# Two attention items in flight, projections one unit ahead, row normalisation moved to ScalarE

## The reference

```python
x = L0_attn_hidden_states
xn = _layernorm(x, axis=-1)
s = _L0_attn_ref(xn, L0_attn_wq, L0_attn_wk, L0_attn_wv, L0_attn_wo)
g = _silu(_L0_ffn_ref(xn, L0_ffn_router_w, L0_ffn_A, L0_ffn_B))
x = x + s * g
...
q = q * cos + _rotate_half(q) * sin
k = k * cos + _rotate_half(k) * sin
...
scores = scores * scale
scores = scores + causal.astype(dt)
probs = jax.nn.softmax(scores.astype(jnp.float32), axis=-1).astype(dt)
attn = jnp.einsum('bhqk,bhkd->bhqd', probs, v)
```

## Time and profile before

| | |
|---|---|
| time, median of 3 runs | 1474.9 us (1472.89 to 1476.49) |
| span of the profiled execution | 1473.0 us |
| PE matmul busy | 1372.8 us (93%) |
| DVE busy | 1196.0 us (81%) |
| ACT busy | 809.3 us (55%) |
| POOL busy | 423.0 us (29%) |

### The profile page before, as it was taken

The page is one execution under the profiler, slowest core; times in us unless marked ns, Lnnn a source line. Parts: engine busy times, 40 slices in busy tenths (PEclk is TensorE's granted clock), DMA queues, the critical chain, the costliest instruction groups (busy, mean ns, idle before and its releaser), DMA issues.

```text
span 1473.0 us, 23326 instructions
## 1 busy us (share of the span) xinstructions
PE 1372.8 (93%) x6982; PEld 1130.1 (77%) x6982; DVE 1196.0 (81%) x3022; ACT 809.3 (55%) x2064; POOL 423.0 (29%) x340
## 2 busy tenths in 40 slices
PE   6699999999998999989999999999999999999997
PEld 5577667788777887778777887778877787877785
DVE  6976768878889887888888788887787888888887
ACT  4445555555555665556555555556555565555563
POOL 4311123221434123241342213331233312423231
PEclk9799999999999999999999999999999999999999
DMA  5000021000001000000000000000000000001223
GB/s 196 22 12 1 22 72 65 22 7 0 21 21 28 0 7 21 14 28 0 14 28 21 7 0 21 21 28 0 2 26 14 28 0 14 22 13 64 79 71 136
DMA packets 23291, 43.33 MB, mean 29 GB/s; under 512 B 2464, under 2 KB 2592, under 8 KB 23264
## 3 DMA queue, kind: packets, MB, share of 16 engines
q1 hardware_dynamic: 20736, 37.90, 8.0%
q10 hardware_dynamic: 2528, 5.11, 0.9%
HBM read 34.61 MB, written 8.39 MB: 29 GB/s over the span
## 4 chain that ended last, share of the span: by engine, by line
PE 49%; issue 21%; DVE 18%; POOL 8%; ACT 3%; DMA 0%; POOLq 0%; DVEq 0%; ACTq 0%
PE o_ps L542 13%; PE bank_b L450 12%; PE bank_a L450 7%; PE s_ps L517 5%; PE pv_ps L532 4%; POOL rot L366 3%; DVE probs L1126 3%; PE t_ps L625 3%; POOL w_lo L359 3%; DVE probs L1079 2%; POOL w_hi L356 2%; PE s_ps L512 2%; DVE cosx L999 2%; DVE cosx L989 2%; DVE q_lo L1005 2%
## 5 line engine op out<-in xcount | busy, mean ns | idle before, releaser
L366 POOL TENSOR_TENSOR rot<-rot,tab 128x512 f32<-128x512 f32 x160 | 209.6, 1310 | 921.3 <-ACT rot L730 921.3
L800 ACT ACTIVATE probs<-probs,row_min 128x128 f32<-128x128 f32 (+1 forms) x512 | 227.1, 445 | 122.1 <-DVE row_min L1079 120.9
L1126 DVE TENSOR_SCALAR probs<-probs,row_inv 128x128 f32<-128x128 f32 (+1 forms) x512 | 208.5, 470 | 4.5
L450 PE MATMUL bank_b<-xT_hi,w_hi 128*128 (+1 forms) x508 | 205.3, 404 | 0.5 <-POOL w_lo L373 0.5
L542 PE MATMUL o_ps<-w_hi,attn_hi 128*128 128x512 f32 x500 | 198.9, 398 | 7.2 <-POOL w_lo L359 4.0
L450 PE MATMUL bank_b<-xT_hi,w_lo 128*128 (+1 forms) x508 | 199.8, 393 | 0.0
L450 PE MATMUL bank_b<-xT_lo,w_hi 128*128 (+1 forms) x508 | 199.2, 392 | 0.0
L542 PE MATMUL o_ps<-w_lo,attn_hi 128*128 128x512 f32 x500 | 197.3, 395 | 0.0
L542 PE MATMUL o_ps<-w_hi,attn_lo 128*128 128x512 f32 x500 | 196.8, 394 | 0.0
L761 ACT ACTIVATE attn_hi<-pv_ps 128x512 fp32r<-128x512 f32 x128 | 76.4, 597 | 172.1 <-PE pv_ps L532 171.3
L625 PE MATMUL t_ps<-tab,probs 128*128 128x128 f32 x768 | 110.9, 282 | 49.1 <-DVE probs L1126 49.0
(11 more groups left out here) (151 smaller groups left out, 3094.8 us busy)
## 6 DMA issues: line engine op xcount, KB each, us to landing
raw<-w_seq SPq DMA_DIRECT2D x78, 256.0 KB, 2.6
gate_scratch<-silu ACTq DMA_DIRECT2D x16, 256.0 KB, 2.1
out<-y_sum SPq DMA_DIRECT2D x16, 256.0 KB, 2.0
raw<-x SPq DMA_DIRECT2D x13, 256.0 KB, 2.7
raw<-gate_scratch SPq DMA_DIRECT2D x13, 256.0 KB, 2.9
x_sb<-x SPq DMA_DIRECT2D x3, 1024.0 KB, 10.6
x_sb<-x SPq DMA_DIRECT2D x4, 256.0 KB, 5.7
tab<-tables ACTq DMA_DIRECT2D x1, 768.0 KB, 5.3
```

Of the source, the lines that this page charges most:

```text
L366: nc.gpsimd.tensor_tensor(v, v, tab[:, s:s + SEQ].unsqueeze(1).to_broadcast([P, 2, SEQ]), ALU.mult).then_inc(sin_done[kind], 1)
L450: mm = nc.tensor.matmul(dst, w(a, c), x[:, c, bass.ds(x0, BLOCK)], start=(c == 0 and n == 0), stop=(c == DC - 1 and n == 2))
L800: a = nc.scalar.activation(s, s, ACT.Exp, bias=row_min[:, i:i + 1], scale=-1.0, accum_out=row_sum[:, i:i + 1])
L1126: ins = nc.vector.tensor_scalar(s, s, row_inv[:, i:i + 1], None, ALU.mult)
```

## The change

The bank pairs `s_ps` and `t_ps` become `pair[0]` and `pair[1]`: the scores of item j and its turned rows share `pair[j % 2]`, and `probs` and `row_min` are doubled. So scores are made two items ahead. All six projections of a unit are made in the unit before. The output tile follows two items behind, not three. The four row normalisations per item move from DVE (`tensor_scalar`) to ACT (`normalise_rows`, an activation with the row's inverse as its scale). K's high part and V's parts are made in one instruction each, not two. The gate steps stand only at places 0 and 3 of an item (after the turning, and at the item's end), over units 0 to 5, and seven units are written out.

```diff
+WRITTEN = 7
...
-        places = [(0, 1, 3)] + [(0, j, p) for j in (2, 3) for p in (0, 1, 3)]
...
+        later = [(u, j, p) for u in range(2, WRITTEN) for j in range(4) for p in (0, 3)]
...
-        s_ps = pb("s_ps", [P, 2, 512])
-        t_ps = pb("t_ps", [P, 2, 512])
+        pair = [pb("pair0", [P, 2, 512]), pb("pair1", [P, 2, 512])]
```

POOL's `group`:

```diff
-                        if i == 0 and j == 2:
-                            pool.wait_ge(proj_done[VT1], own)
-                            split(g, WO)
-                            split(g, WO + 1)
-                        if j > 0 and not last:
-                            sin_product((K, H0)[j - 1] if j < 3 else H1, ahead)
...
+                        if j == 1:
+                            if i == 0 and not first:
+
+                                pool.wait_ge(o_done, value(pool, 4 * u0))
+                                split(g, WO)
+                            if not last:
+                                sin_product(H0, ahead)
+                            if i == 0 and not first:
+                                split(g, WO + 1)
+                            if not last:
+                                sin_product(H1, ahead)
...
+                        if (i, j) == (2, 1):
                             pool.wait_ge(proj_done[K], used)
                             split(g_next, WK)
...
+                            pool.wait_ge(proj_done[H0], used)
+                            split(g_next, WQ)
+                        elif (i, j) == (2, 2):
...
+                            split(g_next, WQ + 1)
+                        elif (i, j) == (2, 3):
...
+                            split(g_next, WQ + 2)
                             pool.wait_ge(proj_done[H3], used)
                             split(g_next, WQ + 3)
```

TensorE's item j of a unit:

```diff
+                pe.wait_ge(probs_ready, n4[j + 1])
+                turn_probs(j)
                 pe_side(u, j, 0)
...
+                        project(K, bank_a, WK, x_next, w_next)
...
+                        project(H1, bank_a, WQ + 1, x_next, w_next)
...
+                        project(H3, bank_a, WQ + 3, x_next, w_next)
...
+                        project(V, bank_b, WV, x_next, w_next)
+                pe_side(u, j, 1)
+
+                pe.wait_ge(pT_ready, n4[j + 1])
+                if j < 2 or not last:
+                    if j == 2:
                         for kind in (K, H0, H1):
                             pe.wait_ge(q_ready[kind], c2)
...
+                    scores((j + 2) % 4)
...
+                prob_value(j)
...
+                    output_heads(b, t, o_ps, range(GROUP), weights=w_own if j == 2 else None).then_inc(o_done, 1)
...
+                        project(H0, bank_b, WQ, x_next, w_next)
...
+                        project(H2, bank_b, WQ + 2, x_next, w_next)
...
+                pe_side(u, j, 3)
```

ScalarE:

```diff
+        def normalise_rows(j, done):
+            act = nc.scalar
+            act.wait_ge(inv_done, done)
...
+                    a = nc.scalar.activation(s, s, ACT.Copy, scale=row_inv[:, i:i + 1])
+            a.then_inc(probs_ready, 1)
...
+                if j == 1 and not last:
+                    k_high(c2, n4[4])
+                    q_high(H0, c2, n4[3])
...
+                if not end:
+                    normalise_rows((j + 1) % 4, n4[j + 2])
```

VectorE:

```diff
-                        ins = nc.vector.tensor_scalar(s, s, row_inv[:, i:i + 1], None, ALU.mult)
-                ins.then_inc(probs_ready, 1)
...
+                elif j == 1 and not last:
+                    rotate(H0, c2)
+                    cos_product(H1, bank_a, c2)
```

More of the change, by code:

```diff
@@ L61, with loop @@
 KINDS = ["k", "h0", "h1", "h2", "h3"]
-BUF = {K: 0, H0: 1, H1: 0, H2: 1, H3: 1}
-V, VT0, VT1 = 5, 6, 7
+BUF = {K: 0, H0: 1, H1: 0, H2: 1, H3: 0}
+V = 5
+WRITTEN = 7
+FINAL = UNITS - BLOCKS
+LAST = UNITS - 1
+def loop(eng, first, end, body):
+    with eng.Fori(first, end) as i:
+        body(i)
 def build(nc, x, w_seq, a_r, b_t, tables, out):
@@ L154, in build @@
         x0_in = [sem(f"x0_in{t}") for t in range(BLOCK_TILES)]
+        land_in = [sem(f"land_in{c}") for c in range(len(landing))]
         ar_in = sem("ar_in")
@@ L238, in build @@
             through_ps += what in THROUGH
-        assert len(places) >= len(steps)
-        SIDE_X = TILES - X_FIRST
+        assert all(at < (3, 2, 0) for at, (what, _, _) in side_plan.items() if what in ("x", "ar", "mt", "route", "exp"))
         def side_uses(u, j, p):
@@ L279, in value, with slots, units @@
             return v if isinstance(v, int) else eng.snap(v)
+        def slots(eng, u):
+            return {c: value(eng, 4 * u + c) for c in range(-2, 8)}
+        def units(eng, u):
+            return [value(eng, u + c) if c else u for c in range(3)]
         @block.sync
@@ new lines, in group @@
+                        if g_next is None and 4 * i + j > 2:
+                            add_residual(4 * i + j - 3, (4 * i + j - 3) % 2)
+                        if j == 0 and not last:
+                            sin_product(K, ahead)
+                        if j == 0 and i == 0 and first:
+                            inverse_std(2)
+                        if j == 1:
[8 more added lines that the diff above has]
+                                sin_product(H1, ahead)
+                            if i == 0 and first:
+                                inverse_std(3)
+                                split(g, WO)
+                                split(g, WO + 1)
@@ new lines, in act_unit @@
+                if j == 1 and not last:
+                    k_high(c2, n4[4])
+                    q_high(H0, c2, n4[3])
+                elif j == 2 and not last:
+                    q_high(H2, c2, n4[4])
+                if not end:
+                    normalise_rows((j + 1) % 4, n4[j + 2])
+                attn_high(j, n4[j + 1], None if first and j < 3 else n4[(-2, -2, 0, 0)[j]])
+                act_side(u, j, 2)
+                act_side(u, j, 3)
+                if is_unit(u, last_d[0]) and j == last_d[1]:
+                    store_silu(TILES - 1)
@@ L1094, in dve_unit @@
-                dve_side(u, j, 0)
-                if j == 0:
-                    q_low(H2, c1)
-                    if first:
-                        for t in range(BLOCK_TILES, 2 * BLOCK_TILES):
-                            x_low(t, first_banks[t % BLOCK_TILES])
-                elif j == 2 and not last:
-                    k_low(0, c2)
-                elif j == 3 and not last:
-                    q_low(H0, c2)
-                if not (first and j == 0):
-                    turned_low(n)
@@ L1157, in dve_unit @@
-                dve_side(u, j, 2)
+                elif j == 3 and not last:
+                    q_low(H3, c2)
+                if not end:
+                    row_inverse(n4[j + 2])
+                if j == 0 and not last:
+                    cos_product(K, bank_a, c2, H3, c1)
+                elif j == 1 and not last:
+                    rotate(H0, c2)
+                    cos_product(H1, bank_a, c2)
+                elif j == 2 and not last:
+                    rotate(H2, c2)
+                    cos_product(H3, bank_a, c2, H1, c2)
@@ new lines, in dve_unit @@
+                if first and j == 0:
+                    block_statistics(2)
+                elif first and j == 1:
+                    block_normalise(2)
+                    block_statistics(3)
+                elif first and j == 2:
+                    block_normalise(3)
+                if is_unit(u, 1) and j == 2:
+                    split_ar()
+                dve_side(u, j, 1)
+                if j < 2 or not last:
+                    mask_rows((j + 2) % 4, n4[j + 3])
+                if j == 0 and not last:
+                    rotate(K, c2)
+                elif j == 1 and not last:
+                    k_low(c2)
+                    q_low(H0, c2)
+                    rotate(H1, c2)
+                elif j == 2 and not last:
+                    q_low(H2, c2)
+                    rotate(H3, c2)
```

763 lines of the change are left out of this document (345 added, 418 removed).

## The result

The changed kernel takes 1561.8 us (median of 4 runs, 1560.98 to 1563.99) where the kernel before takes 1474.9: 1.0597 times as long, 95% interval 1.0582 to 1.0612. The forecast was 1535, slower, in a range of 1455 to 1575. The direction was right and 27 us were missing. The profiled execution has a span of 1559.2 us, and what follows is reckoned on it.

What follows compares the result with a forecast made beforehand. TensorE was taken as nearly matmul-bound, losing time where weights are split. First turning 43.5, units 0 to 6 378, units 7 to 30 1072 and end 39.5 gave 1533 us span, 1535 median; range 1455 to 1575.

Steps and rivals of the forecast that it cites:

- Clean unit: Unit without weight splits: 39.7 us of matmul stream plus 1.4 waiting for H1's low part, 41.1 (40.6 to 41.5).
- First unit: First unit of a group: POOL's sine behind a split awaiting the output tile costs 11 us over clean (6.5 to 13).
- ScalarE's normalisation: Four row normalisations per item moved from DVE to ScalarE: 1.4 us there, between 1.0 and 2.0.
- Third unit: Third unit of a group, where five chunks are split: 4 us over a clean unit, bounds 1 and 7.
- The rival in which the port costs little: DVE slips between POOL's instructions; first unit costs 6.5, third 1 to 2, gate 66: 1480 to 1495 us; chance 0.20.
- The rival in which the clock falls in each unit: The 1.4 us wait in every unit lowers TensorE's clock, losing 1.7 us each: 1578 us; chance 0.08.
- The gate: Gate steps in units 0 to 6: 56 us before plus 1.1 for each of 19 pairs, 77 (56 to 95).
- The first turning: Stretch from the start to TensorE's first turning: 43.5 us, as before.
- The last unit: Last unit and end, without projections to hide the parts behind: 39.5 us, where 38.1 before.

Runs made afterwards that it cites:

- Experiment 1: Changed kernel, with POOL making H0's and H1's sine products before it waits for the output tile and splits two output chunks in a group's first unit: 1503.5 us.
- experiment 2: Changed kernel with the four row normalisations back on DVE, directly behind the reciprocal: 1591.8 us.
- mended kernel: Kernel 9: (8) with the next group's splits K in third unit, H0 to H3 in fourth's long items, V in its item 2; routing in unit 3: 1467.2 us.
- (11): The mended kernel with the four row normalisations back on DVE: 1494.2 us.
- (3): The kernel before, with only the four row normalisations moved to ScalarE, directly after the exponentials: 1576.8 us.
- (5): Experiment 1 with the last twenty gate steps at places 0 and 1 of an item, not 0 and 3: 1496.9 us.
- (8): Experiment 1 with all gate steps but one at places 0 and 1, x's first transposes one item later, first gate tiles one item after routing: 1479.5 us.
- Kernel 12: The mended kernel with K's split in item 0 of the third unit, H0's behind K's sine product, V's in item 1 of the fourth: 1472.5 us.

## Why the forecast was right in direction and 27 us short

**Clean unit: right.** 41.1 forecast, 41.1 measured. In a clean unit's item 2, DVE's low part of H1 and the scores that wait for it:

```profile
918.38 1.28 POOL L361 TENSOR_TENSOR rot<-rot,tab 128x512 f32<-128x512 f32 x1 [6.71 <-ACT rot L713]
...
919.01 1.19 DVE L1003 TENSOR_TENSOR q_lo<-cosx,q_hi 128x512 fp32r<-128x512 f32 x1
...
920.35 0.36 PE L515 MATMUL pair<-k_parts,q_hi 128*128 128x256 f32 x1 [1.36 <-DVE q_lo L1003]
```

POOL's sine ends at 919.66 and DVE's subtraction 0.54 later, 1.19 us long where 0.7 is the mean in the kernel before. The Trainium skill (SBUF — State Buffer, Who interferes with whom) says that a VectorE instruction with two SBUF inputs contends with a GpSimd instruction that reads SBUF, and the trace agrees again: 4 of the 128 low parts of Q took over 0.9 us in the kernel before and 37 in the changed one, and POOL was at work at the start of every one of them.

**First unit: right, link by link.** ScalarE, DVE and POOL from item 1 of a first unit on:

```profile
860.08 1.04 POOL L346 TENSOR_TENSOR w_hi<-raw,zero 128x512 fp32r<-128x512 f32 x1 [13.67 <-PE o_ps L544]
861.20 1.29 POOL L349 TENSOR_TENSOR w_lo<-raw,w_hi 128x512 fp32r<-128x512 f32 x1
862.45 1.26 POOL L361 TENSOR_TENSOR rot<-rot,tab 128x512 f32<-128x512 f32 x1
```

```profile
865.28 0.63 ACT L720 ACTIVATE q_hi<-cosx 128x512 fp32r<-128x512 f32 x1 [7.00 <-DVE cosx L997]
865.82 1.48 ACT L767 ACTIVATE probs<-probs,row_inv 128x128 f32<-128x128 f32 x4
```

```profile
863.74 1.51 DVE L997 TENSOR_TENSOR cosx<-cosx,rot 128x512 f32<-128x512 f32 x1 [7.39 <-POOL rot L361]
...
870.77 1.80 DVE L1003 TENSOR_TENSOR q_lo<-cosx,q_hi 128x512 fp32r<-128x512 f32 x1
```

TensorE's turning of item 1 is at 851.36. From there: the split begins at 8.7 (forecast 8.7), the rotation ends at 13.9 (14.0), ScalarE's normalisation at 15.9 (16.0), TensorE has stood 4.72 us (4.8). The scores come at 877.42, which is 26.1 (near 26), after 4.84 us (some 6; the projection before them ran partly at the lower clock). The unit costs 11.8 over a clean one (11). Experiment 1 shows that the order makes 8.8 of it.

Of the 11.8 us, 8.2 are longer waits (4.72, and 4.84 where a clean unit has 1.37). The remaining 3.6 go with the lower clock: over this unit the granted clock is 0.90, where it is 1.00 in kernel 1's first unit and in a clean one. So some 3.6 of the 8.8 us that the bad order costs are the clock that falls with the waits, of which the prediction counted 1.6 (an estimate by subtraction).

How much of the second wait is contention and how much is DVE's late start was not measured apart.

**ScalarE's normalisation: right.** 1.4 forecast, 1.48 measured, and the Trainium skill's rule (ScalarE: Activation LUTs, Rules for kernel authors) that multiplications belong on VectorE costs 30 us here when it is followed (experiment 2) and 27 in the mended kernel (11). In the kernel before it is right by 102 us (3). As the traces read, which engine is the better one depended on what stood behind the instruction in the queue, not on its length.

**Third unit: right,** 4.3 of 4. **The rival in which the port costs little** falls: in the first unit the rotation and the low part of H0 met POOL and took 1.51 and 1.80 us, and even without the bad order (experiment 1) such a unit costs 3 us over a clean one. **The rival in which the clock falls in each unit** falls too: the granted clock is 1.00 from 893 to 945, through a whole clean unit with its wait of 1.36. In the loop it falls only in first and third units (0.950 over the whole run, where the kernel before has 0.972).

**The gate: the term that was mis-sized.** At the loop's prices units 0 to 6 come to 7 x 41.15 - 5.6 + 11.8 + 2 x 4.3 = 302.9, so the gate cost 394.7 - 302.9 = 92 us, where the sum had 77 and its upper bound 95. I counted 1.1 us for each pair of steps and nothing for what stands ahead of a step in DVE's queue. The pair itself was sized right: at 225.58 and 228.20 the two steps wait 0.35 and 0.69 us. But setting ten pairs apart (5) brought 4.5 us in units 0 to 6 and not 12, so what remains of the 92 is not all pairs. Three steps waited for DVE's queue (TensorE, wait in brackets):

```profile
75.67 0.69 PE L456 MATMUL o_ps<-tab,x_sb 128*128 128x128 f32 x2 [10.05 <-DVE xT_lo L903]
...
214.10 1.03 PE L491 MATMUL o_ps<-tab,mid 128*64 128x128 f32 x4 [11.44 <-DVE mid L980]
...
319.91 1.22 PE L495 MATMUL o_ps<-bT_full,gmT_full 64*128 64x512 f32 x1 [10.64 <-DVE y_sum L1061]
```

The first stands behind DVE's statistics and norms, the second behind the routing, the third, in the first unit of a group, behind the rotation that waits for POOL: there the wait of the loop's first unit and the gate's pair fall on each other. The three make 32 us; in the kernel before, the longest such waits were 5.1 and 1.9. Moving the steps apart (8) and the routing to a unit without splits, together with the new places of the splits (9), brought units 0 to 6 from 380.8 in kernel 1 to 361.4 and 351.1, the time of the kernel before.

**The small terms.** The first turning came at 45.2, not 43.5: its normalisation now stands behind ScalarE's copy of the second item's scores, and with the normalisation on DVE (experiment 2) it is 43.5 again. Units 29 and 30 take 42.2 (1517.51 - 1475.30), 1 us each, which I had left out: in item 3 TensorE waits 0.89 us for a low part of Q, which stands behind the gate's multiplication of an output tile in DVE's queue. The last unit took 41.7, not 39.5. Of the 26 us of span that the sum lacked, units 0 to 6 hold 16.7, the six later first units 2, units 29 and 30 another 2, start and end 1.7 and 2.2, and 0.05 us in each unit the rest.

**What stays open.** Kernel 9 keeps 1.3 us in its third and in its fourth unit, and its turnings place both in item 3 (10.2 us from turning to turning where a clean one has 8.9), with a wait of 1.16 for a low part of Q. A split that POOL makes in item 2 stands before each of them, H0's in the third unit and V's in the fourth. Kernel 12, in which H0's isn't there and V's ends early in the item, takes 8.9 in both. What the single instructions for K and V and the earlier projections brought was not tried apart. Nor was it tried to make TensorE's output tile independent of the split in another way, as by a second copy of the output weights, or to place the splits of the kernel before anew.

## What to carry to other kernels

Look for the instruction in an in-order queue that waits for the engine that sets the pace, and write down everything behind it: one such wait ahead of two sine products cost 58 of the 87 us. A place in a program is a time only if something holds the engine there; work with no wait in front of it runs at once, and falls where the neighbour is busy. Whether a move from one engine to another pays hangs on what it delays behind it: the same edit cost 102 us in one order and saved 30 in the other. And a gain in the body of the loop can be lost at its ends: of the 15 us that kernel 9 wins in units 7 to 30, 8 reach the time.

## What was not expected of the hardware

The granted clock's share in a wait was larger than reckoned. Otherwise nothing is new. DVE's and POOL's instructions alternated on two-input operations in the stretches read here as in the kernel before (a low part of Q 0.7 us alone, up to 1.80 beside POOL). The granted clock fell with TensorE's long waits, between its two levels of 1.2 and 2.4 GHz: the 5 us from 868, right after the wait of 4.72, have 0.69, and the 5 us around the wait of 4.84 have 0.65. The clean stretch at 893 has 1.00 (windows of the changed kernel; PE, PEld, DVE, ACT, POOL busy us, PEclk, DMA share, GB/s).

```profile
873.00:878.00 5.00, 0.58 (x3) 0.61 (x4) 5.00 (x9) 3.56 (x11) 2.34 (x3) 0.65 0.16 52
893.00:898.00 5.00, 5.00 (x33) 4.45 (x32) 2.52 (x4) 4.32 (x12) 0.00 (x0) 1.00 0.00 0
```
